# New places in a hand-written schedule: 72 of 564 side jobs of a fused attention and feed-forward kernel move by a fraction of a step to six steps

## The chip, the cores and the metric

The kernel runs on one core of one Trainium2 chip. The metric is the device time in microseconds of one execution, as the median of the runs. The engines are named as in the profile: PE is TensorE's matmul side and PEld its weight loads, DVE is VectorE, ACT is ScalarE, POOL is GpSimd, and SP (or SPq) is SyncE, which issues every DMA of this kernel.

## The reference

Four batches of 1024 tokens of 256 channels, each with a context of 77 tokens, go through one cross-attention layer and one feed-forward layer:

```python
# x: (4, 1024, 256), ctx: (4, 77, 256), 16 heads of 16
h   = layernorm(x)
q   = h @ Wq
kv  = concat(ctx, h) @ Wkv                 # 1101 keys
dots = einsum(q, k) * 16 ** -0.5           # key j is hidden where j > i + 77
x   = x + (softmax(dots) @ v) @ Wout + bout
h   = layernorm(x)
h   = block_quant(h) @ block_quant(w_fc).T + b_fc      # 1024 hidden units, blocks of 32, 3 mantissa bits
h   = gelu(h)
out = x + block_quant(h) @ block_quant(w_proj).T + b_proj
```

`block_quant` rounds each block of 32 values to three mantissa bits under the exponent of the block's largest value.

## The kernel before, in words

**Attention sets the beat.** The work is cut into 196 steps, 48 for each of the first three batches and 52 for the last. A batch has two parts of 512 queries (the last batch: 512, 256 and 256), a part has four groups `g` of four heads (a block), and a block has a step for every 512 columns of key tiles. In each step PE multiplies keys with queries into the four banks of `psS` in two pairs (L1239), ACT takes the exponential of each pair into `probs` (L722), POOL zeroes what the mask hides (L665), and PE multiplies `probs` with the values into `psO` (L1224), one step behind, and two steps behind for the first step of a block.

**psO is one bank.** All steps of a block add up in it. When the block is done DVE copies it out (L992, item `o`: transpose, reciprocal, product, and for odd groups a second transpose into `attT`). The first product of the next block waits for that copy (`pe.wait_ge(o_copied, st.block)`, L1220). It stands in PE's loop two iterations after the block's last step, and everything behind it on PE waits with it.

**Side jobs.** All else is an item of a plan: `ln1`, `ln1root`, `ln1end` (first layer norm), `xnT` and `ctxT` (transposes), `qk` (projections, rounded into three bf16 parts by ACT, by DVE and POOL in `mid`, and laid out by `stack`'s DMAs), `v`, `over` and `flag` (a guard against overflow), `wout` (output projection and residual), `ln2`, `ln2root`, `ln2end` (second layer norm), `q2` and `q2end` (quantization of its result into `hq`'s first half), `xqT` (its transpose), `fc` (eight half tiles in one go, GELU by ACT, L795), `hamax` and `hq` (quantization of a hidden tile by DVE, L861 to L873), `hT` (a DMA transpose by SP, L623), `proj` (second projection, L1168, added to the residual by DVE, L1054), `store`, and the preparation of the weights (`lateloads`, `wquant`, `wload`, `wT`).

**The order is written by hand.** `PLACES` (L189 to L229) has a table for each batch. A number is the step before or after the batch's first at which the item is put; a negative one lies in the batch ahead. `plan()` (L233) sorts all items by that number and puts each into the first half (`PLAN[k, 0]`) or the second half (`PLAN[k, 1]`) of iteration `k`. Every engine walks the same plan in program order and does its share of each item:

```python
# PE, iteration k (L1254 to L1280)
score_pair(k + 1, 0); handle PLAN[k, 0]; score_pair(k + 1, 1); pv of PV_AT[k]; handle PLAN[k, 1]
# DVE, POOL and SP, iteration k
handle PLAN[k, 0] + PLAN[k, 1]
# ACT, iteration k (act_plan, L295): ctxT, xnT, v and qk stand one half later
exp(k + 1, 0); first half; exp(k + 1, 1); second half
```

So a number in `PLACES` sets two things: where in PE's stream of score and value products an item stands, and the order of items on each of the other engines. No engine passes an item that waits. Items that need PSUM take turns in three banks `psD` (`places()`, L310): `qk` has the third for itself after the start, `fc` goes round all three, the others alternate between two. PE waits until the one who read a bank last has freed it.

Two waits of SP matter below. `hT` of tile n waits until DVE has written `hq` of that tile and until PE has finished the `proj` that read the buffer before (`bank_full`, L622). `store` waits until DVE has added the result of its `proj` (`bank_free`, L626). SP runs its items in order as well.

Of the kernel before, what the change touches and what calls it, by code (L numbers as in the profile page):

```python
# [174 lines left out]
def diagonal(seg):  # L175
# [11 lines left out]
DONE_BEFORE = {"over": 1, "flag": 1, "xnT": 2, "ln1": 1, "ln1root": 1, "ln1end": 1, "v": 2}  # L187

PLACES = (  # L189
    {"lateloads": (6,), "ln1": (0,), "ln1root": (.5,), "ln1end": (1,), "xnT": (4, 4.5), "qk": (5.5, 7, 9, 11),  # L190
     "mid": (6.5, 8.5, 10, 12.5), "over": (13.35,), "flag": (13.35,), "stack": (8.6, 13), "v": (13.5, 16.25, 17.25),
     "o": (5, 9, 13, 17, 25, 32.75, 41, 49), "wquant": (14.5, 19, 29.1, 30.4), "wload": (17.25,),
     "wT": (22.5, 22.75, 23.5, 24.5, 32.25, 32.75, 33, 35), "xres": (7, 27.9),
     "xresb": (14.5, 15.5, 16, 17, 36, 37, 38, 39), "wout": (17, 20.75, 50.5, 51.25), "ln2": (22.75, 52),
# [14 lines left out]
     "proj": (40, 44, 69, 73.85), "store": (41, 44.1, 74, 74.75)},  # L209
    {"xin": (-67.5, -67.5), "cin": (-42,), "ctxT": (-31.85,), "ln1": (-63,), "ln1root": (-59,), "ln1end": (-57.25,),  # L210
     "xnT": (-44, -39.75, -36, -31), "qk": (-24, -20.95, -18, -14.5, -10, -4.5, -1.95, 5, 9.5),
     "mid": (-22.5, -19, -17, -11, -8, -2.25, 0, 7, 11), "over": (-7, 13.5), "flag": (-5.5, 13.75),
     "stack": (-15.5, -1, 2, 13), "v": (-15, -6.5, .5, 6, 0), "o": (5, 9, 13, 17, 25, 33, 41, 49), "xres": (7, 28),
     "xresb": (14.5, 15.5, 16.5, 17.5, 35.75, 37, 38, 39), "wout": (17.5, 20.25, 49.5, 52), "ln2": (23.75, 52),
# [4 lines left out]
     "store": (41, 44.1, 71.5, 74.75)},  # L219
    {"xin": (-67.5, -67.5), "cin": (-42,), "ctxT": (-31.85,), "ln1": (-59,), "ln1root": (-59,), "ln1end": (-53.25,),  # L220
     "xnT": (-44, -39.75, -36, -31), "qk": (-24, -20.95, -18, -14.5, -9.5, -4.6, -1.95, 5, 9.5),
     "mid": (-22.5, -19, -17, -11, -7.5, -2.25, 0, 7, 11), "over": (-7, 13.5), "flag": (-5.5, 13.75),
     "stack": (-15.5, -1, 2, 13), "v": (-15, -6.5, .5, 6, 0), "o": (5, 9, 13, 17, 21, 25, 29, 33, 38, 43, 48, 53),
     "xres": (7, 27.5), "xresb": (14.5, 15.5, 16.5, 17.5, 30, 31, 32, 33), "wout": (17.5, 21.25, 33, 54),
# [1084 lines left out]
```

How the kernel before makes its waits and increments, by code:

```python
        def flag_of(eng, b, c):  # L491
            eng.wait_ge(flag_ready, CHUNKS * b + c + 1)
            n = CHUNKS * b + c
            return eng.value_load(flag_i[0:1, n:n + 1], min_val=0, max_val=1) > 0
# [38 lines left out]
            def stack(b, c, hf):  # L534
                before = [((b - 1) * CHUNKS + 1) * GROUPS + 2 * hf + 1, 2 * (2 * (CHUNKS * b + c) + hf - QB) + 1]
                if max(before) > 0:
                    sp.wait_ge(pair_scored, 2 * (BLOCK_END[max(before)] + 1))
                lo, hi = (0, FIRST_KEYS) if c == 0 else (CTX, FIRST_KEYS)
                sp.wait_ge(parts_ready, NUMBER["qk", b, c, "q", hf] + 1)
                for s in range(SLOTS):
                    sp.dma_start(q_stack[DH * s:DH * (s + 1), q_place(b, c, hf), :, :],
                                 q_parts[:, hf, Q_PART[s], :]).then_inc(stacked[hf], 16)
                sp.wait_ge(parts_ready, NUMBER["qk", b, c, "k", hf] + 1)
                for s in range(SLOTS):
                    sp.dma_start(k_stack[DH * s:DH * (s + 1), HH * hf:HH * (hf + 1), CHUNK * c + lo:CHUNK * c + hi],
                                 k_parts[:, hf, K_PART[s], lo:hi]).then_inc(stacked[hf], 16)
# [1 line left out]
            def place_guard(k, guarded):  # L549
                st = STEPS[k]
                with sp.If(guarded):
                    sp.wait_ge(guard_split, (st.block + 1) * 4)
                    for s in range(3):
                        sp.dma_start(q_heads(GUARD + s, GUARD + s + 1, st)[:, :, st.at:st.at + st.nq],
```

## Time and profile before

| what | value |
|---|---|
| runs | 661.85, 661.31 and 658.93 us, median 661.31 us |
| profiled execution, own time | 661.85 us |
| its span in the profile | 660.1 us |
| mean granted clock of TensorE | 0.944 |
| busy: PE, DVE, ACT, POOL | 574.1, 430.6, 422.3, 219.9 us |

The span runs from the first to the last instruction of the profiled execution, and 1.75 us of that execution's time lie outside it. Busy shares are means over the whole span: the kernel begins with some 36 us ahead of the first exponential and ends with some 35 us of the last tiles' feed-forward after the last one, and in both PE is often idle. "Granted clock" is the share of full speed that TensorE was allowed; the page's row of clocks has it per slice.

### The profile page before, as it was taken

The page shows a single profiled execution, that of the slowest core. Times are in us where ns is not written, and L with a number is a line of the kernel's source. Part 1 is how long each engine was busy: PE and PEld are TensorE (multiplying, and loading weights), DVE is VectorE, ACT ScalarE, POOL GpSimd, SP SyncE. Part 2 cuts the span into 40 slices and gives each one's busy share as a digit, 9 for nine tenths or more (in the row PEclk, how much of TensorE's full clock was granted, in tenths as well). Part 3 has the DMA queues.
Part 4 walks back from the last instruction along what each step waited for, and adds up shares of the span by engine and source line. Part 5 has one row for each costly group of instructions (what it writes and reads, how often), then busy time and mean ns, then how long its engine had stood idle before and what let it go on. Part 6 is the DMA issues. An engine that isn't in the chain of part 4 may idle for free.

```text
span 660.1 us, 11818 instructions
## 1 busy us (share of the span) xinstructions
PE 574.1 (87%) x4147; PEld 268.0 (41%) x4147; DVE 430.6 (65%) x925; ACT 422.3 (64%) x555; POOL 219.9 (33%) x313
## 2 busy tenths in 40 slices
PE   8469789999998899998898799999999888898743
PEld 4213344333463335334354334444353355454321
DVE  4503877999848477679545677667239779584655
ACT  3156557678757686787456686887667845965800
POOL 3314511534325412524333611424336514212100
PEclk9969889999999899999899999999999989897976
DMA  5997902360099712347199612139199504111102
GB/s 143 122 132 180 142 8 97 87 83 17 17 136 116 147 28 55 112 72 82 49 110 143 81 18 65 49 55 113 47 121 145 68 17 98 18 34 49 33 16 49
DMA packets 77703, 52.04 MB, mean 79 GB/s; under 512 B 37771, under 2 KB 77319, under 8 KB 77626
## 3 DMA queue, kind: packets, MB, share of 16 engines
q1 hardware_dynamic: 77626, 51.02, 49.0%
q8 instruction: 47, 0.77, 0.6%
q14 instruction: 30, 0.25, 0.2%
HBM read 12.12 MB, written 4.19 MB: 25 GB/s over the span
## 4 chain that ended last, share of the span: by engine, by line
PE 49%; DVE 28%; issue 8%; ACT 5%; DMA 4%; SPq 3%; POOL 1%; DVEq 0%; ACTq 0%; POOLq 0%
PE psO L1224 14%; PE psS L1239 13%; PE psD L1139 4%; PE psD L1105 4%; DVE hid L872 4%; ACT probs L722 4%; PE psD L1159 3%; DMA k_stack<-k_parts 3%; DVE amax L861 3%; PE psD L1115 3%; PE psD L1168 3%; DVE hq L873 2%; DVE o_cols L992 2%; PE psD L1157 2%; DVE hid L853 2%
## 5 line engine op out<-in xcount | busy, mean ns | idle before, releaser
L722 ACT ACTIVATE probs<-psS 128x1024 f32<-128x1024 f32 (+4 forms) x392 | 329.4, 885 | 180.4 <-PE psS L1239 179.2
L1239 PE MATMUL psS<-q_stack,k_stack 99*128 99x512 bf16 (+5 forms) x1008 | 200.4, 315 | 21.9 <-ACT probs L722 8.4
L665 POOL TENSOR_SCALAR_AFFINE_SELECT probs<-probs 128x512 f32<-128x512 f32 (+2 forms) x164 | 106.2, 659 | 334.1 <-ACT probs L722 334.0
L1224 PE MATMUL psO<-probs,v_aug 128*17 128x512 f32 (+5 forms) x2016 | 177.5, 458 | 8.3 <-DVE o_cols L992 4.9
L1239 PEld LDWEIGHTS psS<-q_stack,k_stack 99*128 99x128 bf16 (+1 forms) x1008 | 80.9, 103 | 150.5 <-ACT probs L722 75.6
L1224 PEld LDWEIGHTS psO<-probs,v_aug 128*17 128x17 f32 (+1 forms) x2016 | 43.7, 97 | 93.3 <-issue 75.7
L861 DVE TENSOR_REDUCE amax<-hid 128x32 f32<-128x1024 f32 (+1 forms) x45 | 53.4, 1187 | 27.4 <-ACT hid L795 26.6
L872 DVE TENSOR_TENSOR hid<-hid,magic 128x1024 f32<-128x1024 f32 (+1 forms) x45 | 55.6, 1235 | 9.0 <-DMA hT<-hq 4.0
L873 DVE TENSOR_TENSOR hq<-hid,magic 128x1024 bf16<-128x1024 f32 (+1 forms) x41 | 53.8, 1312 | 1.4
L992 DVE STREAM_TRANSPOSE o_cols<-psO 128x512 f32<-128x512 f32 (+1 forms) x36 | 23.5, 654 | 47.7 <-PE psO L1224 47.1
L795 ACT ACTIVATE hid<-psD 128x512 f32<-128x512 f32 x64 | 36.8, 597 | 22.8 <-PE psD L1159 21.0
L1115 PE MATMUL psD<-wv,xcT 128*128 128x256 f32 (+1 forms) x160 | 40.4, 397 | 2.6 <-DVE k_most L946 2.1
L1139 PE MATMUL psD<-wo,attT 128*128 128x256 f32 x128 | 34.0, 412 | 9.1 <-DVE attT L1001 9.0
L1159 PE MATMUL psD<-wfc,xqT 128*128 128x512 bf16 x128 | 41.7, 410 | 0.0
L1168 PE MATMUL psD<-wproj,hT 128*128 128x256 bf16 x256 | 32.6, 281 | 8.3 <-DMA hT<-hq 8.3
L1105 PE MATMUL psD<-xcT,wk 128*128 128x512 f32 (+1 forms) x96 | 34.8, 492 | 0.0
L1115 PEld LDWEIGHTS psD<-wv,xcT 128*128 128x128 f32 (+1 forms) x160 | 29.7, 191 | 11.0 <-DVE k_most L946 2.9
L1006 DVE TENSOR_TENSOR x<-psD,x 128x512 f32<-128x512 f32 x16 | 11.1, 691 | 34.3 <-PE psD L1139 34.3
L1105 PE MATMUL psD<-xcT,wq 128*128 128x512 f32 x64 | 30.7, 601 | 1.2 <-ACT xcT L735 1.2
L1139 PEld LDWEIGHTS psD<-wo,attT 128*128 128x128 f32 x128 | 24.9, 202 | 16.6 <-issue 13.0
L1168 PEld LDWEIGHTS psD<-wproj,hT 128*128 128x128 bf16 x256 | 25.1, 100 | 14.7 <-issue 6.4
L945 DVE TENSOR_TENSOR rest<-psD,k_parts 128x512 f32<-128x512 f32 (+1 forms) x20 | 12.3, 614 | 28.2 <-ACT k_parts L775 27.5
(91 smaller groups left out, 546.7 us busy)
## 6 DMA issues: line engine op xcount, KB each, us to landing
q_stack<-q_parts SPq DMA_DIRECT2D x96, 128.0 KB, 4.8
k_stack<-k_parts SPq DMA_DIRECT2D x48, 147.2 KB, 7.8
k_stack<-k_parts SPq DMA_DIRECT2D x48, 128.0 KB, 5.5
x_in<-in_x_dram SPq DMA_DIRECT2D x8, 512.0 KB, 5.2
x<-in_x_dram SPq DMA_DIRECT2D x8, 512.0 KB, 5.3
out_dram<-x SPq DMA_DIRECT2D x16, 256.0 KB, 2.2
hid<-in_L_ffn_w_fc_dram SPq DMA_DIRECT2D x1, 1024.0 KB, 6.5
hid<-in_L_ffn_w_proj_dram SPq DMA_DIRECT2D x1, 1024.0 KB, 4.9
```

The source lines that it names most:

```text
L665: last = pool.affine_select(out=tile, in_=tile, compare_op=ALU.is_ge, fill=0.0, base=first - (P * t - CTX), pattern=[[0, GH], [1, m]], cha ...
L722: act.activation(probs[:, k % PB, 2 * pair:2 * pair + 2, 0:n], psS[:, 2 * pair:2 * pair + 2, 0:n], ACT.Exp, scale=DH ** -0.5).then_inc(pro ...
L861: chain(s, dve.tensor_reduce(size, v.rearrange("p (a k) -> p a k", k=BLK), AXX, ALU.max, apply_absolute_value=True), c0 + 1)
L872: chain(s, dve.tensor_tensor(vb, vb, const, ALU.add), c0 + 4)
L873: return dve.tensor_tensor(q.rearrange("p (a k) -> p a k", k=BLK), vb, const, ALU.subtract)
L1105: last = pe.matmul(dst, wt[:, kk, f * P:(f + 1) * P], xcT[:, kk, src:src + size], start=(kk == 0), stop=(kk == KD - 1))
L1115: last = pe.matmul(ps[0:rows, D * a:D * (a + 1)], xcT[:, kk, first:first + rows], wv[:, kk, :], start=(kk == 0), stop=(kk == KD - 1))
L1139: last = pe.matmul(ps[:, D * (t % 2):D * (t % 2 + 1)], attT[:, kk, P * (t % SUB):P * (t % SUB + 1)], wo[:, kk, :], start=(kk == 0), stop=( ...
L1159: last = pe.matmul(ps[:, :], xqT[:, t % SUB, kk, :], wfc[:, kk, cols], start=False, stop=(kk == KD - 1))
L1168: last = pe.matmul(ps[:, D * (t % 2):D * (t % 2 + 1)], hT[:, t % 2, kk, :], wproj[:, kk, :], start=(kk == 0), stop=(kk == KH - 1))
L1224: last = pe.matmul(psO[SQ * j:SQ * j + VW, first - st.q0:first - st.q0 + n], v_aug[0:rows, v_tile(st.b, st.c, t), GH * st.g + j, :], probs ...
L1239: last = pe.matmul(psS[0:rows, j, off:off + n], k_stack[0:ROWS, GH * st.g + j, P * t:P * t + rows], q_heads(0, ROWS, st)[:, j, first - CHU ...
```

## The change

Only numbers in `PLACES` change. No instruction is added or removed, no shape and no buffer changes; eight items swap the two shared PSUM banks. The diff, cut to the numbers that the prediction speaks of:

```diff
-    {"lateloads": (6,), "ln1": (0,), "ln1root": (.5,), "ln1end": (1,), "xnT": (4, 4.5), "qk": (5.5, 7, 9, 11),
+    {"lateloads": (2,), "ln1": (0,), "ln1root": (.5,), "ln1end": (1,), "xnT": (3, 4), "qk": (5, 7, 9, 11),
...
-     "o": (5, 9, 13, 17, 25, 32.75, 41, 49), "wquant": (14.5, 19, 29.1, 30.4), "wload": (17.25,),
+     "o": (5, 9, 13, 17, 28, 33, 41, 49), "wquant": (14.5, 19, 28.2, 29.5), "wload": (16.25,),
...
-     "x1b": (27, 28, 29, 30, 56, 57, 58, 59), "xqT": (30, 36.4, 58, 61), "fc": (37.5, 62),
+     "x1b": (27, 28, 29, 30, 56, 57, 58, 59), "xqT": (36, 36.5, 58, 61), "fc": (37.5, 62),
...
-     "store": (47.2, 50.5, 70, 75.5)},
+     "store": (47.1, 50.5, 70, 75.5)},
...
-     "qk": (-24, -20.95, -17.5, -14.5, -10, -6.75, .05, 5, 9), "mid": (-22.5, -20, -17, -12, -8, -2, 2, 6.9, 11),
+     "qk": (-24, -20.95, -17.5, -14.5, -10, -7, -1.45, 5, 9), "mid": (-22.5, -20, -17, -12, -8, -2, .5, 7, 11),
...
-     "o": (5, 9, 13, 17, 25, 33, 41, 49), "xres": (7, 28), "xresb": (14.5, 15.5, 16.5, 17.5, 36, 37, 38, 39),
+     "o": (5, 9, 13, 17, 28, 33, 41, 49), "xres": (7, 28), "xresb": (14.5, 15.5, 16.5, 17.5, 36, 37, 38, 39),
...
-    {"xin": (-67.5, -67.5), "cin": (-42,), "ctxT": (-31.85,), "ln1": (-63,), "ln1root": (-59,), "ln1end": (-57.25,),
+    {"xin": (-67.5, -67.5), "cin": (-42,), "ctxT": (-32,), "ln1": (-59,), "ln1root": (-59,), "ln1end": (-53.25,),
...
```

What that does to the order, by absolute step (`o(0,1,0)` is batch 0, second part, first group; "a" and "b" are the two halves of an iteration):

| items | before | after | passes on DVE or SP |
|---|---|---|---|
| `lateloads` | 6a | 2a | SP: ahead of both `xin` of batch 1 |
| `xnT(0,2)`, `xnT(0,3)`, `qk(0,1,q,0)` | 4a, 4b, 5b | 3a, 4a, 5a | nothing |
| `o(0,1,0)` | 25a | 28a | DVE: goes behind `mid`, `ln2end` and `q2` |
| `xqT(0,0)` | 30a | 36a | DVE: behind both `wquant` |
| `ln1(2)`, `ln1end(2)` | 33a, 38b | 37a, 42b | DVE: behind `xqT(0,1)`; behind `hamax(0,1)` |
| `qk`, `mid(1,1,k,0)` | 48a, 50a | 46b, 48b | PE: `qk` ahead of `proj(0,0)` |
| `store(0,0)` | 47a, after `hT(0,3)` | 47a, before it | SP: ahead of `hT(0,3)` |
| `mid(1,1,q,1)` | 54b | 55a | DVE: behind `ln2end(0,1)` and `q2(0,1)` |
| `o(1,1,0)` | 73a | 76a | DVE: behind `ln2root`, `proj(0,3)`, `mid`, `ln2end` and `q2` |
| `hq(1,5)` | 113b | 114a | DVE: behind `wout(2,0)` |
| `hq(2,5)` | 160a | 162a | DVE: behind `o(3,0,3)` and `wout(3,0)` |
| `wout(3,1)` | 165a | 164a | DVE: ahead of `hamax(2,7)` and `o(3,1,0)` |
| `hamax(3,1)`, `wout(3,2)` | 176b, 177a | 178a, 178b | DVE: `hamax` behind `o(3,1,3)` |
| `hq(3,3)`, `proj(3,0)` | 182b, 182b | 183a, 184a | DVE: `proj` behind `ln2end(3,1)` |
| `hamax(3,5)`, `hq(3,5)` | 191b, 192b | 192a, 193a | DVE: `hamax` behind `o(3,2,2)` |
| `proj(3,2)` | 196, after `wout(3,3)` | 195b | PE: ahead of the last value product and of `wout(3,3)` |

The remaining moved items shift by a half step or one step and keep their order on DVE, ACT, POOL and SP, apart from `wT`, `fc` and `xnT` items of the same kind as above and `store(1,2)`, which goes ahead of `hT(1,7)`.

## Rows read from the trace of the kernel before

**Rows 1.** The list of waits, whole span: who waited for whom, us, times, longest.
```profile
PE psD L1148 <- DVE hq L873: 20.0, 7, 7.6
...
PE psO L1224 <- DVE o_cols L992: 4.9, 2, 3.8
```
**Rows 2.** Timeline of DVE around step 27: start, us, what, [idle before].
```profile
117.30 0.72 DVE L992 STREAM_TRANSPOSE o_cols<-psO 128x512 f32<-128x512 f32 x1
...
119.25 1.58 DVE L853 TENSOR_SCALAR hid<-x,mean,rs 128x256 f32<-128x256 f32 x4
...
122.67 1.23 DVE L872 TENSOR_TENSOR hid<-hid,magic 128x1024 f32<-128x1024 f32 x1
```
**Rows 3.** Timeline of PE, same stretch and a little on.
```profile
118.16 1.91 PE L1224 MATMUL psO<-probs,v_aug 128*17 128x512 f32 x16 [1.01 <-DVE o_cols L992]
...
136.40 0.38 PE L1130 MATMUL psD<-ident_b,hid 128*128 128x128 bf16 x4 [1.03 <-DVE hid L873]
```
**Rows 4.** Timeline of DVE, steps 73 to 76.
```profile
260.00 0.72 DVE L992 STREAM_TRANSPOSE o_cols<-psO 128x512 f32<-128x512 f32 x1 [1.54 <-PE psO L1224]
...
264.73 1.59 DVE L853 TENSOR_SCALAR hid<-x,mean,rs 128x256 f32<-128x256 f32 x4
...
268.16 1.23 DVE L872 TENSOR_TENSOR hid<-hid,magic 128x1024 f32<-128x1024 f32 x1
```
**Rows 5.** Timeline of PE, steps 74 to 77.
```profile
263.64 1.91 PE L1224 MATMUL psO<-probs,v_aug 128*17 128x512 f32 x16
...
270.99 0.38 PE L1148 MATMUL psD<-ident_b,hq 128*128 128x128 bf16 x4 [1.26 <-DVE hq L873]
```
**Rows 6.** One window: length; busy (count) of PE, PEld, DVE, ACT, POOL; clock; DMA share; GB/s.
```profile
212.00:221.00 9.00, 5.64 (x26) 1.50 (x26) 5.43 (x8) 2.21 (x5) 6.70 (x7) 0.63 0.81 154
```
**Rows 7.** Timeline of SP and PE, steps 47 to 49.
```profile
180.92 2.62 SPq L623 DMA_TRANSPOSE hT<-hq  x2
...
187.64 1.91 PE L1168 MATMUL psD<-wproj,hT 128*128 128x256 bf16 x16
```
**Rows 8.** Instructions on tile hT: from issue to landing.
```profile
DMA to landing us min/median/max: 1.7/3.1/8.1
```
**Rows 9.** Timeline of DVE and PE, steps 55 to 59.
```profile
204.33 0.69 DVE L945 TENSOR_TENSOR rest<-psD,q_parts 128x512 f32<-128x512 f32 x1 [1.23 <-ACT q_parts L775]
...
215.36 0.59 PE L1148 MATMUL psD<-ident_b,hq 128*128 128x128 bf16 x4 [3.61 <-DVE hq L873]
```
**Rows 10.** Timeline of DVE and PE, steps 160 to 173.
```profile
529.04 0.70 DVE L992 STREAM_TRANSPOSE o_cols<-psO 128x512 f32<-128x512 f32 x1
...
531.38 3.44 PE L1139 MATMUL psD<-wo,attT 128*128 128x256 f32 x8 [2.42 <-DVE attT L1001]
...
560.38 0.61 PE L1148 MATMUL psD<-ident_b,hq 128*128 128x128 bf16 x8 [2.20 <-DVE hq L873]
```
**Rows 11.** Timeline of DVE and PE, steps 175 to 188.
```profile
571.25 1.21 DVE L861 TENSOR_REDUCE amax<-hid 128x32 f32<-128x1024 f32 x1
...
577.18 1.97 PE L1139 MATMUL psD<-wo,attT 128*128 128x256 f32 x8 [1.05 <-DVE attT L1001]
...
600.44 0.69 DVE L1054 TENSOR_TENSOR x<-psD,x 128x512 f32<-128x512 f32 x1 [1.62 <-PE psD L1168]
...
603.97 0.58 PE L1148 MATMUL psD<-ident_b,hq 128*128 128x128 bf16 x4 [2.70 <-DVE hq L873]
```
**Rows 12.** Timeline of DVE, SP and PE, step 191 to the tail.
```profile
616.28 7.09 SPq L623 DMA_TRANSPOSE hT<-hq  x2
...
618.58 0.45 DVE L992 STREAM_TRANSPOSE o_cols<-psO 128x256 f32<-128x256 f32 x1 [0.77 <-PE psO L1224]
...
627.60 1.97 PE L1139 MATMUL psD<-wo,attT 128*128 128x256 f32 x8 [1.71 <-DVE attT L1001]
...
631.98 0.69 DVE L1054 TENSOR_TENSOR x<-psD,x 128x512 f32<-128x512 f32 x1
```
**Rows 13.** Timeline of PE, step 4.
```profile
48.21 0.39 PE L1239 MATMUL psS<-q_stack,k_stack 99*128 99x512 bf16 x1 [2.67 <-issue]
```

More of the change, by code:

```diff
@@ L189 @@
 PLACES = (
-    {"lateloads": (6,), "ln1": (0,), "ln1root": (.5,), "ln1end": (1,), "xnT": (4, 4.5), "qk": (5.5, 7, 9, 11),
-     "mid": (6.5, 8.5, 10, 12.5), "over": (13.35,), "flag": (13.35,), "stack": (8.6, 13), "v": (13.5, 16.25, 17.25),
-     "o": (5, 9, 13, 17, 25, 32.75, 41, 49), "wquant": (14.5, 19, 29.1, 30.4), "wload": (17.25,),
-     "wT": (22.5, 22.75, 23.5, 24.5, 32.25, 32.75, 33, 35), "xres": (7, 27.9),
-     "xresb": (14.5, 15.5, 16, 17, 36, 37, 38, 39), "wout": (17, 20.75, 50.5, 51.25), "ln2": (22.75, 52),
+    {"lateloads": (2,), "ln1": (0,), "ln1root": (.5,), "ln1end": (1,), "xnT": (3, 4), "qk": (5, 7, 9, 11),
+     "mid": (6.5, 8.5, 10, 12.5), "over": (13.25,), "flag": (13.25,), "stack": (8.6, 13), "v": (13.5, 16.25, 17.75),
+     "o": (5, 9, 13, 17, 28, 33, 41, 49), "wquant": (14.5, 19, 28.2, 29.5), "wload": (16.25,),
+     "wT": (22.5, 22.75, 23.5, 24.5, 32.25, 32.75, 33, 35), "xres": (7, 28),
+     "xresb": (14.5, 15.5, 16, 17, 36, 37, 38, 39), "wout": (17, 21, 50.5, 51.25), "ln2": (23.75, 52),
@@ L195 @@
      "ln2root": (24.75, 54), "ln2end": (26, 55), "q2": (27, 55), "q2end": (28, 58),
[1 row of a table removed]
[1 row of a table added]
      "hamax": (39, 42, 44, 45.25, 62, 64, 67, 69), "hq": (40, 43, 45, 46.5, 63, 66, 68, 70),
[1 row of a table removed]
-     "store": (47.2, 50.5, 70, 75.5)},
-    {"xin": (-43.5, -43.5), "cin": (-41.5,), "ctxT": (-26.1,), "ln1": (-36, -28.25), "ln1root": (-36, -26),
-     "ln1end": (-30.25, -25.5), "xnT": (-29, -22.5, -22, -19.75),
-     "qk": (-24, -20.95, -17.5, -14.5, -10, -6.75, .05, 5, 9), "mid": (-22.5, -20, -17, -12, -8, -2, 2, 6.9, 11),
-     "over": (-7.75, 12.5), "flag": (-7.75, 13.75), "stack": (-15.5, 2, 2, 13), "v": (-16.75, -6, .5, 6, -5),
-     "o": (5, 9, 13, 17, 25, 33, 41, 49), "xres": (7, 28), "xresb": (14.5, 15.5, 16.5, 17.5, 36, 37, 38, 39),
[4 rows of a table removed]
-     "proj": (40, 44, 69, 73.85), "store": (41, 44.1, 74, 74.75)},
@@ L210 @@
-    {"xin": (-67.5, -67.5), "cin": (-42,), "ctxT": (-31.85,), "ln1": (-63,), "ln1root": (-59,), "ln1end": (-57.25,),
-     "xnT": (-44, -39.75, -36, -31), "qk": (-24, -20.95, -18, -14.5, -10, -4.5, -1.95, 5, 9.5),
[1 row of a table added]
+     "store": (47.1, 50.5, 70, 75.5)},
+    {"xin": (-43.5, -43.5), "cin": (-41.5,), "ctxT": (-26.25,), "ln1": (-36, -28.25), "ln1root": (-36, -26),
+     "ln1end": (-30.25, -25.5), "xnT": (-29, -23, -22, -21.25),
+     "qk": (-24, -20.95, -17.5, -14.5, -10, -7, -1.45, 5, 9), "mid": (-22.5, -20, -17, -12, -8, -2, .5, 7, 11),
+     "over": (-7.75, 12.5), "flag": (-7.75, 13.75), "stack": (-15.5, 2, 2, 13), "v": (-16.75, -6, .5, 6, -5),
+     "o": (5, 9, 13, 17, 28, 33, 41, 49), "xres": (7, 28), "xresb": (14.5, 15.5, 16.5, 17.5, 36, 37, 38, 39),
[4 rows of a table added]
+     "proj": (40, 44, 69, 73.75), "store": (41, 44.1, 70, 74.75)},
@@ L212 @@
+    {"xin": (-67.5, -67.5), "cin": (-42,), "ctxT": (-32,), "ln1": (-59,), "ln1root": (-59,), "ln1end": (-53.25,),
+     "xnT": (-44, -39.75, -36, -31), "qk": (-24, -20.95, -18.5, -14.5, -10, -4.75, -1.95, 5, 9.5),
      "mid": (-22.5, -19, -17, -11, -8, -2.25, 0, 7, 11), "over": (-7, 13.5), "flag": (-5.5, 13.75),
@@ L214 @@
      "xresb": (14.5, 15.5, 16.5, 17.5, 35.75, 37, 38, 39), "wout": (17.5, 20.25, 49.5, 52), "ln2": (23.75, 52),
[4 rows of a table removed]
[L219 to L222, printed above, removed]
-     "stack": (-15.5, -1, 2, 13), "v": (-15, -6.5, .5, 6, 0), "o": (5, 9, 13, 17, 21, 25, 29, 33, 38, 43, 48, 53),
-     "xres": (7, 27.5), "xresb": (14.5, 15.5, 16.5, 17.5, 30, 31, 32, 33), "wout": (17.5, 21.25, 33, 54),
[3 rows of a table removed]
-     "hT": (32.5, 35.5, 40.1, 40.15, 47.5, 49), "proj": (38.5, 42.75, 54), "store": (41, 44, 54.5)},
[4 rows of a table added]
+     "store": (41, 44.1, 70.5, 74.75)},
+    {"xin": (-67.5, -67.5), "cin": (-42,), "ctxT": (-32,), "ln1": (-59,), "ln1root": (-59,), "ln1end": (-53.25,),
+     "xnT": (-44, -39.75, -36, -31), "qk": (-24, -20.95, -18.5, -14.5, -10, -4.75, -1.95, 5, 9.5),
+     "mid": (-22.5, -19, -17, -11, -8, -2.25, 0, 7, 11), "over": (-7, 13.5), "flag": (-5.5, 13.75),
+     "stack": (-15.5, -1, 2, 13), "v": (-15, -6.5, .5, 6, 0), "o": (5, 9, 13, 17, 21, 25, 29, 33, 38, 43, 48, 53),
+     "xres": (7, 27.5), "xresb": (14.5, 15.5, 16.5, 17.5, 30, 31, 32, 33), "wout": (17.5, 20.25, 34.5, 54),
[3 rows of a table added]
+     "hT": (32.5, 35.5, 40.1, 40.15, 47.5, 49.5), "proj": (40, 42.75, 51.5), "store": (41, 44, 52)},
 )
```

24 rows, old and new, of the table PLACES are left out of this document.

## The prediction

> **What bounds the kernel now.** I read the list of waits first, then the timelines of PE and DVE side by side at each place where the plan changes. PE is the engine that seldom rests: it is busy for seven eighths of the span, and between the first exponential and the last nearly every idle microsecond of it has a name. The longest of those names in this case are two: PE waits for DVE to finish quantizing the second layer norm before it can transpose it (seven waits, 20.0 us together, the longest in the tail), and twice for DVE's copy of the attention accumulator, 4.9 us [rows 1]. So PE's stream of products sets the pace, and a place costs time where DVE or a DMA is late for it. A stall on PE is not made up later as long as PE's stream is dense, because the same products still follow.
>
> A stall also has a tail. After a wait of 2.42 us the eight output projections took 3.44 us; the same eight took 1.97 us elsewhere [rows 10, 12]. The granted clock says why: over 212 to 221 us, around a wait of 3.61 us, it averaged 0.63, so most of that stretch ran at 1.2 GHz instead of 2.4 [rows 6, 9]. After waits of 1.01 us sixteen products still took 1.91 us [rows 3, 5]. I take 1.5 us for such a tail, from 3.44 less 1.97, with 0 and 3.3 us as its ends (9.0 us at 0.63 loses 0.37 of 9.0).
>
> **The accumulator's copy, batch 0.** `o(0,1,0)` goes from 25 to 28, but the value product that waits for it stays in iteration 26. DVE now does `mid`, `ln2end` and `q2` first. In the trace DVE began this copy at 117.30, right after the work ahead of it, `ln2end` at 119.25 and the first pass of `q2end` at 122.67 [rows 2]. From 119.25 to 122.67 lie `ln2end` and `q2`, 3.42 us, and `mid` takes what lies between the copy's group (1.5 us) and 119.25, 0.45 us: the copy starts 3.9 us later. `wout(0,1)` goes behind one pair of scores, on which DVE waits, 0.5 us more. PE idled 1.01 us before; it will idle 5.4 us, 4.4 us more, and the tail adds 1.5. Behind the waiting product stand all scores, so ACT starves as well, and nothing covers it. Against it: PE is then late for DVE, so the wait of 1.03 us for `wquant` [rows 3] goes, but `ln1(2)` now stands at 37 and pushes `over` and `flag(1,0)` back by roughly 0.6 us. Sum +5.5 us, bounds +2.5 (only the copy's move less both short waits) and +8.
>
> **The same in batch 1.** Here DVE was not late: it stood idle for 1.54 us until the block was done, and began the copy at 260.00 [rows 4]. Now `ln2root`, `proj(0,3)`, `mid`, `ln2end` and `q2` come first. `ln2root` fits ahead of the block's end, but `proj(0,3)` binds: PE ends it after 262.8, then follow its addition and `mid` (1.05 us between 263.68 and 264.73), then 3.43 us of `ln2end` and `q2` [rows 4]. With `ln2root` out of the way the addition starts at 262.9, so the copy starts at 267.4 and ends at 268.2. PE wanted it at 263.64 [rows 5]: 4.6 us. The wait of 1.26 us at `xqT` a little later [rows 5] goes, since `q2end` then ends ahead of PE. With the tail, 4.6 - 1.3 + 1.5 = +4.8 us, bounds +2.3 and +6.5.
>
> The Trainium skill ("TensorE: Matmul & The Clock Gate", "HAM oscillation") puts the cost of a throttled stretch at its duration times one less 1.2/2.4, and says in "What's actually happening" that the affected matmuls vary from run to run with the phase of the monitor. By that rule the two tails together would lie anywhere between nothing and what two such stretches cost; the trace agrees with the size (clock 0.63) and shows no run-to-run variation, having one execution. My sum keeps the row's 1.5 us each.
>
> **SP around step 47.** `store(0,0)` goes ahead of `hT(0,3)`, so `hT(0,3)` waits for DVE's addition of `proj(0,0)` and one more issue; and `qk(1,1,k,0)`, four products and 1.9 us, goes ahead of `proj(0,0)` on PE, which delays all of SP against PE's stream. Both `hT` were issued from 180.92 to 183.54, one takes 3.1 us to land, and `proj(0,1)` wanted the second buffer in its second half, near 188.6 [rows 7, 8]. New: 183.5 + 1.9 + 1.7 + 3.1 = 190.2, up to 1.7 us late. DVE's later position can hide nothing here. Bounds 0 and +3; I take +1.0, between the two, as the landing may be as fast as the least in rows 8.
>
> **Waits that shrink.** `mid(1,1,q,1)` goes behind `ln2end` and `q2`. DVE stood 1.23 us for ACT at that point with the whole chain to `q2end` behind it, and PE waited 3.61 us for that chain [rows 9]. I take -1.2 us, bounds 0 and -3 (half of the slow stretch in rows 6 goes too). `hq(2,5)` goes behind `o(3,0,3)`: the block was done about 1.3 us before the copy began at 529.04, so the wait of 2.42 us shrinks to 1.1 and its slow stretch of 1.5 us goes [rows 10]. But the next wait, 2.20 us at 560.38, is for DVE's own chain [rows 10], which is ahead by only the 0.6 us that it idled less. So what PE gains in between it waits out there: -0.6 us, bounds 0 and -2.9.
>
> **Last batch, steps 176 to 188.** `wout(3,2)` goes half a step and more later and loses its wait of 1.05 us. `hamax(3,1)` (1.21 us and two small operations, 1.6 together, begun at 571.25) no longer fills the time in which DVE waited for the block; it is done before `wout`, but `hq(3,1)` stands behind the addition of `wout(3,2)`, which PE now reaches after two more pairs of scores and 32 value products, near 580.6 instead of 577.18: `hq(3,1)` ends about 3.5 us later. From there to 600.44 DVE had only 1.62 us to spare, and its chain ends in the wait of 2.70 us at 603.97 [rows 11]. 3.5 - 1.6 = 1.9, and `hT(3,3)` may bring 1 more: +2.0 us, bounds 0 and +3.5.
>
> **Tail.** `proj(3,2)` stood behind `wout(3,3)`, where PE had nothing else, and its addition (0.69 us at 631.98) stood in DVE's chain. Now it stands ahead of the last value product and waits for `hT(3,5)`. That was issued at the end of the SP row, 622.14 with 1.23 us; `hamax(3,5)` now starts behind `o(3,2,2)` (618.58 and 1 us) instead of ahead of it, which moves it by some 1.7 us [rows 12]. With 3.1 us to land [rows 8] that is 626.9; half of `proj`, 1 us, the last value product, 0.3, and the copy with two transposes, 1.65, put `wout(3,3)` at 629.9 instead of 627.60 [rows 12]. Less 0.7 for the addition: +1.6 us, bounds -0.7 and +3.
>
> **Steps 2 to 6.** A megabyte of `w_fc` is now moved while the key and query stacks of the second head half still land. PE's wait of 2.67 us in the middle of one pair of scores has no releaser in the program [rows 13]; it may be code loading, which more traffic would lengthen. Nearest row: that wait itself, so -2.7 to +2.7; I take 0. Everything else (`x1b`, `xresb`, `wT`, `fc` or `qk` by half a step, with equal order on the other engines) moves products within PE's dense stream: 0, bounds -2 and +2.
>
> **Sum.** 5.5 + 4.8 + 1.0 - 1.2 - 0.6 + 2.0 + 1.6 = 13.1 us on the profiled execution's own 661.85 us, 675.0 us. The median lies 0.5 us under it: 674.5 us.
>
> **The rivals.**
> - *The two copies alone* (chance 0.2). The waits are real, but the slow stretches, SP's delay and the last batch's shifts are hidden by waits that are there already: 4.4 - 1.0 + 0.6 + 4.6 - 1.3 = 7.3 us less the 1.8 of the shrinking waits, +5.5, 667 us. For it: DVE often has slack on the way to its next wait (1.62 and 1.54 us). Against it: rows 10 show a wait of half that length with its slow tail.
> - *All ends high* (0.15). The hT after `store` lands late, code loading is delayed, and the last batch pays both: the high bounds of these three, 3 + 2.7 + 3.5, instead of 3.0, make +19.3, 681 us.
> - *Not slower* (0.07). VectorE's chain from `ln2` to `xqT`, and not PE, is the bound between the blocks. Reordering a chain of fixed length costs nothing, PE just waits at `psO` instead of at `xqT`, and only the freed waits count: -1.2 - 2.9 - 1.05, about -5 us, 656 us. It decides where DVE's wait for PE after the copy would vanish by as much as PE's wait grows. For it: DVE had under 0.1 us idle around step 27. Against it: the waits that PE had at `xqT` and `wquant` are 1.26 and 1.03 us [rows 3, 5], a quarter of the new ones.
> - *The numbers do nothing* (0.03), because PE has slack that the modelled ends of its products conceal: 661 us.
>
> The likeliest, 674.5 us, has 0.55. Its own range is 669 to 680; with the neighbours the range is 664.5 to 681.5 us. About 0.5% is what a measurement of this kernel can tell from no change. Faster by over 0.5%: 0.06; within: 0.06; slower: 0.88.
>
> **What the new profile would show.** PE waiting for `o_cols` about 5 us near step 27 and 4 to 5 us near step 76, each with a stretch of clock below 0.7 behind it; the wait for `hq` at `xqT(1,0)` gone; the wait at `wout(3,0)` at about 1.1 us without a slow stretch; the last `wout` about 2 us later after the last exponential. The prediction is wrong if the list of waits has less than 7 us for `psO` on `o_cols`, or if that figure is there and the span has grown by less than 5 us.

## The result, and the profile after

The changed kernel takes 684.44 us (median of 4 runs, 680.23 to 686.13) where the kernel before takes 660.56 us (median of 4, 658.93 to 661.85). The ratio is 1.035, with an interval of 1.030 to 1.041, so it is slower by some 23 us. The forecast was 674.5 us with a range of 664.5 to 681.5: the sign was right, and the time lies above the range. The profiled execution took 684.1 us, its span is 682.3 us and TensorE's mean granted clock in it 0.931, against 660.1 us and 0.944 before.

To place the 22.15 us between the two spans I took the start of the first exponential of every step from both traces and subtracted. Where that lag jumps, the time was lost. It is a safer reading than a span alone, since two executions of one kernel differ by several us (more on that below). The tail counts from the end of the last exponential.

| place | lag it adds, us | predicted |
|---|---|---|
| steps 0 to 27 | +0.9 | 0 |
| steps 28 to 41, copy of batch 0 | +5.4 | +4.9 |
| steps 42 to 58, `flag` and SP | +2.9 | +1.6 |
| steps 59 to 60, `mid(1,1,q,1)` | -3.4 | -1.2 |
| steps 61 to 78, copy of batch 1 | +5.0 | +4.8 |
| steps 79 to 158 | +0.7 | 0 |
| steps 159 to 176, `hq(2,5)` and `xqT(3,0)` | +1.1 | -0.6 |
| steps 177 to 190 | +6.2 | +2.0 |
| tail | +3.4 | +1.6 |
| sum | 22.2 | 13.1 |

The prediction had its 0.6 us for `flag` inside the +5.5 of the first copy (4.4 + 1.5 - 1.0 + 0.6). Here it stands with `flag`, in the row of steps 42 to 58, where its cost falls.

The list of waits of the changed kernel answers [rows 1]; its columns are the same. PE's waits for the accumulator's copy have risen from 4.9 to 17.0 us. These are four waits: 4.73 and 4.58 us at the two moved copies, 3.95 us at step 184, and one of 3.74 us at step 91 that the kernel before had too (3.85 us).

```profile
PE psD L1148 <- DVE hq L873: 21.3, 6, 8.7
PE psO L1224 <- DVE o_cols L992: 17.0, 4, 4.7
```

The group of the value products on the page shows that they are also longer. They overlap, and keep PE busy for 184.3 us where it was 177.5. They are the same 2016 products, some of them at a lower clock.

```profile
L1224 PE MATMUL psO<-probs,v_aug 128*17 128x512 f32 (+5 forms) x2016 | 184.3, 473 | 20.3 <-DVE o_cols L992 17.0
```

**The two copies** stand in the timeline of PE (first fence) and of DVE (second), and answer [rows 2 to 5]. In both places DVE now does `ln2end` and the first half of `q2` (L853, L861) before it copies the accumulator (L992), and PE gets the bank some 0.9 us after the copy's start.

```profile
122.27 3.61 PE L1224 MATMUL psO<-probs,v_aug 128*17 128x512 f32 x16 [4.73 <-DVE o_cols L992]
...
273.98 3.53 PE L1224 MATMUL psO<-probs,v_aug 128*17 128x512 f32 x16 [4.58 <-DVE o_cols L992]
```

```profile
117.99 1.59 DVE L853 TENSOR_SCALAR hid<-x,mean,rs 128x256 f32<-128x256 f32 x4
119.72 1.22 DVE L861 TENSOR_REDUCE amax<-hid 128x32 f32<-128x1024 f32 x1
...
121.40 0.72 DVE L992 STREAM_TRANSPOSE o_cols<-psO 128x512 f32<-128x512 f32 x1
...
268.63 0.69 DVE L1054 TENSOR_TENSOR x<-psD,x 128x512 f32<-128x512 f32 x1 [2.31 <-PE psD L1168]
...
273.11 0.72 DVE L992 STREAM_TRANSPOSE o_cols<-psO 128x512 f32<-128x512 f32 x1
```

After each of the two waits the sixteen products take 3.6 and 3.5 us instead of 1.91. The windows over both places and over a third (columns as in [rows 6]) give the reason, a granted clock of 0.52, 0.62 and 0.57.

```profile
120.00:127.00 7.00, 4.73 (x21) 1.57 (x22) 5.14 (x8) 0.00 (x0) 0.43 (x1) 0.52 0.09 31
273.50:278.00 4.50, 4.03 (x19) 1.00 (x20) 3.46 (x5) 0.00 (x0) 0.00 (x0) 0.62 0.99 333
604.00:612.00 8.00, 3.79 (x36) 1.66 (x36) 7.45 (x18) 1.87 (x3) 2.84 (x2) 0.57 0.01 2
```

**Single waits of PE** that the prediction spoke of, in the order of its timeline: for `flag`'s scale ahead of step 42 (0.56 us before, second fence), at `xqT(0,2)` [rows 9], at `wout(3,0)` and at `xqT(3,0)` [rows 10].

```profile
168.90 0.24 PE L1122 MATMUL psD<-head_sum,qk_most 128*1 128x8 f32 x4 [2.01 <-DVE qk_most L954]
...
223.67 0.38 PE L1148 MATMUL psD<-ident_b,hq 128*128 128x128 bf16 x4 [2.74 <-DVE hq L873]
...
541.77 1.97 PE L1139 MATMUL psD<-wo,attT 128*128 128x256 f32 x8 [1.00 <-DVE attT L1001]
...
571.93 0.58 PE L1148 MATMUL psD<-ident_b,hq 128*128 128x128 bf16 x4 [4.50 <-DVE hq L873]
```

```profile
161.18 0.24 PE L1122 MATMUL psD<-head_sum,qk_most 128*1 128x8 f32 x4 [0.56 <-DVE qk_most L954]
```

**The last batch.** The timelines of PE and of DVE over steps 178 to 189 answer [rows 11]. The wait of 1.05 us at `wout(3,2)` (594.84) is gone. The wait of 2.70 us at `xqT(3,2)` (624.04) is the same to the hundredth. Between them stands a new wait of 3.95 us for the copy of block `o(3,2,0)`.

```profile
594.84 1.99 PE L1139 MATMUL psD<-wo,attT 128*128 128x256 f32 x8
...
608.78 3.38 PE L1224 MATMUL psO<-probs,v_aug 128*17 128x256 f32 x32 [3.95 <-DVE o_cols L992]
...
624.04 0.38 PE L1148 MATMUL psD<-ident_b,hq 128*128 128x128 bf16 x4 [2.70 <-DVE hq L873]
```

```profile
596.93 0.69 DVE L1006 TENSOR_TENSOR x<-psD,x 128x512 f32<-128x512 f32 x1 [5.83 <-PE psD L1139]
597.54 1.53 DVE L872 TENSOR_TENSOR hid<-hid,magic 128x1024 f32<-128x1024 f32 x1
599.10 1.23 DVE L873 TENSOR_TENSOR hq<-hid,magic 128x1024 bf16<-128x1024 f32 x1
600.24 0.74 DVE L824 BATCH_NORM_STATS2 stats<-x 128x6 f32<-128x256 f32 x2
...
605.74 1.23 DVE L872 TENSOR_TENSOR hid<-hid,magic 128x1024 f32<-128x1024 f32 x1
607.00 1.27 DVE L873 TENSOR_TENSOR hq<-hid,magic 128x1024 bf16<-128x1024 f32 x1
608.20 0.44 DVE L992 STREAM_TRANSPOSE o_cols<-psO 128x256 f32<-128x256 f32 x1
```

DVE is never idle for more than 0.1 us from the addition of `wout(3,2)` at 596.93 to the copy at 608.20 (the timeline has 28 instructions there, of which the fence shows the long ones), and the copy is last in the row.

**The tail** on ACT, PE and DVE answers [rows 12]. Each fence is one timeline.

```profile
642.72 0.49 ACT L722 ACTIVATE probs<-psS 128x154 f32<-128x154 f32 x2 [1.04 <-PE psS L1239]
```

```profile
644.46 2.21 PE L1168 MATMUL psD<-wproj,hT 128*128 128x256 bf16 x16
...
646.60 0.33 PE L1224 MATMUL psO<-probs,v_aug 77*17 77x77 f32 x8
...
648.94 3.38 PE L1139 MATMUL psD<-wo,attT 128*128 128x256 f32 x8 [2.02 <-DVE attT L1001]
```

```profile
646.70 0.69 DVE L1054 TENSOR_TENSOR x<-psD,x 128x512 f32<-128x512 f32 x1 [4.20 <-PE psD L1168]
647.31 0.44 DVE L992 STREAM_TRANSPOSE o_cols<-psO 128x256 f32<-128x256 f32 x1
```

### The profile page after: what moved, and what is told of

Same layout as the page of the kernel before. It is cut to its first block, busy times and chain, and to the rows that moved or that the text cites. A ratio compares the mean times of both kernels' runs of the same rounds, so it can differ in the third digit from the quotient of the medians.

```text
span 682.3 us, 11806 instructions
## 1 busy us (share of the span) xinstructions
PE 580.8 (85%) x4138; PEld 269.5 (40%) x4147; DVE 427.4 (63%) x925; ACT 422.0 (62%) x555; POOL 217.9 (32%) x313
## 4 chain that ended last, share of the span: by engine, by line
PE 50%; DVE 27%; issue 8%; DMA 5%; ACT 5%; SPq 3%; POOL 1%; DVEq 0%; ACTq 0%; POOLq 0%
PE psO L1224 15%; PE psS L1239 13%; PE psD L1105 5%; PE psD L1139 4%; DVE hid L872 4%; PE psD L1159 3%; ACT probs L722 3%; DMA k_stack<-k_parts 3%; PE psD L1168 3%; DVE amax L861 3%; PE psD L1115 3%; DVE o_cols L992 2%; DVE hq L873 2%; DVE stats L824 2%; PE psD L1157 2%
## 5 line engine op out<-in xcount | busy, mean ns | idle before, releaser
L1224 PE MATMUL psO<-probs,v_aug 128*17 128x512 f32 (+5 forms) x2016 | 184.3, 473 | 20.3 <-DVE o_cols L992 17.0
L861 DVE TENSOR_REDUCE amax<-hid 128x32 f32<-128x1024 f32 (+1 forms) x45 | 53.4, 1187 | 29.1 <-ACT hid L795 28.2
L992 DVE STREAM_TRANSPOSE o_cols<-psO 128x512 f32<-128x512 f32 (+1 forms) x36 | 23.5, 653 | 47.5 <-PE psO L1224 47.2
L697 POOL TENSOR_TENSOR x<-x,bproj_all 128x256 f32<-128x256 f32 x32 | 23.9, 754 | 24.0 <-DVEq L1023 24.0
```

Of the source, the lines that this page charges most:

```text
L861: chain(s, dve.tensor_reduce(size, v.rearrange("p (a k) -> p a k", k=BLK), AXX, ALU.max, apply_absolute_value=True), c0 + 1)
L1224: last = pe.matmul(psO[SQ * j:SQ * j + VW, first - st.q0:first - st.q0 + n], v_aug[0:rows, v_tile(st.b, st.c, t), GH * st.g + j, :], probs ...
```

## The experiments

Four kernels first, to split the loss by place; then four single edits of the last batch, where the prediction's sum had failed. The kernel before ran beside them, with a median of 661.82 us (7 runs) in the first set and 661.83 us (30 runs) in the second. The kernels of the first set ran four times each, those of the second nine to twelve times. A cost "by the ratio" is the measured ratio less one, times the kernel before.

**1. The changed kernel with both copies back.**

```diff
-     "o": (5, 9, 13, 17, 28, 33, 41, 49), ...      # batches 0 and 1
+     "o": (5, 9, 13, 17, 25, 33, 41, 49), ...
```

> The changed kernel with the two accumulator copies o(0,1,0) and o(1,1,0) put back to 25. Theory A (each copy's move costs its wait and the slow stretch behind it, and nothing recovers it): the profile of the changed kernel lags by 6.0 us at step 28 and 6.3 less 1.2 at steps 76 to 78, so 11 us less than the changed kernel's 684.4: about 673 us, with PE's wait for o_cols near steps 27 and 75 back under 1.1 us. Theory B (other moved items would have cost most of it anyway): 679 us or more.

Measured: 673.76 us, ratio to before 1.018 (1.010 to 1.027). Its span is 670.5 us, 11.8 less than the changed kernel's. Lags against that kernel: -6.2 us at step 28, -6.3 and +1.4 at steps 76 to 78. Its timeline of PE keeps the wait in the last batch:

```profile
530.91 2.99 PE L1139 MATMUL psD<-wo,attT 128*128 128x256 f32 x8 [1.00 <-DVE attT L1001]
...
596.99 3.36 PE L1224 MATMUL psO<-probs,v_aug 128*17 128x256 f32 x32 [3.96 <-DVE o_cols L992]
```

The two copies cost 10.7 us between the medians, as the sum had it, and about half of the loss lies elsewhere. With four runs of each kernel this cost is known to 6 or 7 us only; that it is the copies' rests on the lags, which fall at these two places.

**2. The kernel before with the two copies moved, and nothing else.**

```diff
-     "o": (5, 9, 13, 17, 25, ...                     # batches 0 and 1
+     "o": (5, 9, 13, 17, 28, ...
```

> The kernel before with only the two copies moved from 25 to 28. Theory A: +10 us, about 671 us, both waits between 4 and 5.5 us. Theory B: at most +5.5 us, 666 us.

Measured: 668.09 us, ratio 1.010 (1.005 to 1.016), between the two expectations. Its timeline of PE around step 27:

```profile
124.13 3.58 PE L1224 MATMUL psO<-probs,v_aug 128*17 128x512 f32 x16 [4.91 <-DVE o_cols L992]
```

The lags at the two places are what was predicted (+5.6 at step 28, and +6.8, +0.7 and -1.4 at steps 76 to 78), and the waits too (4.9 and 4.6 us). Yet its runs are only 6.9 us slower, by the ratio, with an interval of 3.2 to 10.6. In the profiled run 3.0 us came back at step 60: the wait at `xqT(0,2)` was 3.05 us instead of 3.61, and no low clock followed. Another 1.2 us came back over steps 159 to 163: `fc` took 1.7 us longer there, and then the wait at `wout(3,0)` was 1.10 us instead of 2.42, with no low clock behind it (more in the last section). The edit doesn't touch these places. The wait at `xqT(0,2)` is 3.05 us in experiments 5 and 8 too, and the one at `wout(3,0)` is 1.10 to 1.24 us in experiments 5 to 7, so I put this down to the execution and not to the edit. Whether the copies cost 7 or 10 us in the kernel before the runs can't tell.

**3. The changed kernel with the last batch's table back.**

```diff
-     "wout": (17.5, 20.25, 34.5, 54), "q2": (26.75, ...), "xqT": (28, 29.25, 43.5), "fc": (29.5, 44.5),
-     "hamax": (31, 34, 36, 38, 46, 48), "hq": (32, 35, 37, 39, 47, 49), "proj": (40, 42.75, 51.5), ...
+     "wout": (17.5, 21.25, 33, 54), "q2": (27.25, ...), "xqT": (28, 28.25, 43.5), "fc": (30, 44.75),
+     "hamax": (31, 32.5, 36, 38, 46, 47.5), "hq": (32, 35, 37, 38.5, 47, 48.5), "proj": (38.5, 42.75, 54), ...
```

> The changed kernel with the last batch's table of the kernel before. In the profiles the last batch accounts for about 10.7 us: 1.1 over steps 159 to 174, 6.2 over steps 178 to 190, 3.4 behind the last exponential. Theory A (the last table's own edits do it): 10 us less than 684.4, about 674 us. Theory B (DVE arrives late in the last batch because hq(2,5) of the third table moved, and the last table only passes it on): under 5 us less, 680 us or more.

Measured: 675.77 us, ratio 1.024 (1.018 to 1.031). The wait at step 184 is gone and the tail is 35.7 us again instead of 39.1. Its list of waits and its timeline of PE at `wout(3,0)` and `xqT(3,0)`:

```profile
PE psO L1224 <- DVE o_cols L992: 13.4, 4, 4.7
```

```profile
541.94 1.97 PE L1139 MATMUL psD<-wo,attT 128*128 128x256 f32 x8 [1.00 <-DVE attT L1001]
...
572.52 1.01 PE L1148 MATMUL psD<-ident_b,hq 128*128 128x128 bf16 x8 [4.50 <-DVE hq L873]
```

The table of the last batch costs 8.7 us in the changed kernel, between the medians. The second fence settles a smaller point: with `hq(2,5)` moved, the wait at `wout(3,0)` falls to 1.00 us and the one at `xqT(3,0)` rises from 2.20 to 4.50 us with the old table of the last batch too. By lag that rise is 4.3 us over steps 166 to 176, where the changed kernel has 3.8.

**4. The kernel before with the last batch's table of the changed one.**

```diff
-     "wout": (17.5, 21.25, 33, 54), "q2": (27.25, ...), "xqT": (28, 28.25, 43.5), "fc": (30, 44.75), ...
+     "wout": (17.5, 20.25, 34.5, 54), "q2": (26.75, ...), "xqT": (28, 29.25, 43.5), "fc": (29.5, 44.5), ...
```

> The kernel before with the last batch's table of the changed kernel. Theory A: +10 us, 671 us, with a wait of about 4 us for o_cols at step 184. Theory B: under +5 us and no such wait.

Measured: 675.96 us, ratio 1.022 (1.016 to 1.027): 14.3 us, more than the 10 expected. In its timeline of PE:

```profile
563.05 0.40 PE L1148 MATMUL psD<-ident_b,hq 128*128 128x128 bf16 x4 [3.62 <-DVE hq L873]
...
598.63 3.62 PE L1224 MATMUL psO<-probs,v_aug 128*17 128x256 f32 x32 [3.58 <-DVE o_cols L992]
```

By lags: +3.3 us over steps 166 to 176, nearly all of it around `xqT(3,0)`, +7.1 up to step 190, +3.4 in the tail. So this table alone does all that the last batch of the changed kernel shows from `xqT(3,0)` on. At `xqT(3,0)` itself it isn't the only cause: experiment 3 has the rise without this table, and with both edits it is no larger (3.8 us). That is one reason why the table costs 14.3 us here and 8.7 in experiment 3, where the rise stays.

**5. `hamax(3,1)` alone.** The kernel before with

```diff
-     "hamax": (31, 32.5, 36, 38, 46, 47.5),
+     "hamax": (31, 34, 36, 38, 46, 47.5),
```

> The kernel before with only hamax(3,1) moved from 32.5 to 34, behind the copy o(3,1,3). Steps 176 to 190 lost 6.2 to 7 us with the whole last table, most of it as a wait of 3.6 to 4.0 us for o_cols at step 184. Theory A (hq(3,1) behind the later wout(3,2) makes DVE late): hamax alone costs 0 to 1.7 us, its own length, and no wait over 1 us at step 184. Theory B (the filling of DVE's idle time by hamax was what kept it in time): +4 us or more, 665 us, with the wait at step 184.

Measured: 661.03 us, ratio 1.000 (0.998 to 1.002). There is no wait at step 184. Its `wout(3,2)` in the timeline of PE:

```profile
578.31 3.57 PE L1139 MATMUL psD<-wo,attT 128*128 128x256 f32 x8 [0.99 <-DVE attT L1001]
```

**6. `wout(3,2)` alone.**

```diff
-     "wout": (17.5, 21.25, 33, 54),
+     "wout": (17.5, 21.25, 34.5, 54),
```

> The kernel before with only wout(3,2) moved from 33 to 34.5. Theory A: hq(3,1) waits behind its addition, ends about 3.5 us later, and PE waits 3 us or more for o_cols at step 184 with a slow stretch behind: +5 us, 666 us. Theory B: PE loses its wait of 1.05 us at the old place and DVE catches up: 0 to -1 us.

Measured: 666.46 us, ratio 1.007 (1.005 to 1.009). Its profiled run is the fastest of its nine, 662.55 us, so the span is no measure of the cost here; the new wait is there. First the timeline of PE, then that of DVE:

```profile
578.92 1.99 PE L1139 MATMUL psD<-wo,attT 128*128 128x256 f32 x8
...
592.61 3.41 PE L1224 MATMUL psO<-probs,v_aug 128*17 128x256 f32 x32 [2.94 <-DVE o_cols L992]
...
606.14 0.58 PE L1148 MATMUL psD<-ident_b,hq 128*128 128x128 bf16 x4 [2.70 <-DVE hq L873]
```

```profile
580.95 0.69 DVE L1006 TENSOR_TENSOR x<-psD,x 128x512 f32<-128x512 f32 x1 [5.61 <-PE psD L1139]
...
592.02 0.44 DVE L992 STREAM_TRANSPOSE o_cols<-psO 128x256 f32<-128x256 f32 x1
```

In the kernel before, the copy and the product that waits for it stand like this, DVE first:

```profile
579.18 0.69 DVE L1006 TENSOR_TENSOR x<-psD,x 128x512 f32<-128x512 f32 x1 [2.15 <-PE psD L1139]
...
590.34 0.44 DVE L992 STREAM_TRANSPOSE o_cols<-psO 128x256 f32<-128x256 f32 x1
```

```profile
591.92 1.92 PE L1224 MATMUL psO<-probs,v_aug 128*17 128x256 f32 x32
```

From the addition to the copy it is 11.2 us before (590.34 - 579.18) and 11.1 us with the edit (592.02 - 580.95). That stretch of DVE is rigid, and how late `wout(3,2)` comes is passed on whole to the copy. PE gets the bank 0.6 us after the copy's start (592.61 - 592.02), so in the kernel before the spare time was 591.92 - 590.34 - 0.6 = 1.0 us.

**7. `proj(3,2)` alone.**

```diff
-     "proj": (38.5, 42.75, 54), "store": (41, 44, 54.5)},
+     "proj": (38.5, 42.75, 51.5), "store": (41, 44, 52)},
```

> The kernel before with only proj(3,2) and its store moved ahead of the last copy and wout(3,3). Theory A (the tail's loss of 3.4 us is proj standing ahead of the last value product): hT(3,5) lands earlier here than in the changed kernel, so the wait is short, and the tail loses proj's own 1.9 us and gives back 0.7 us of DVE: +1 to +2 us between the last exponential and the end. Theory B (what counts is that hT(3,5) is late, by hamax(3,5)'s move): 0.

Measured: 663.30 us, ratio 1.002 (1.000 to 1.004). In the profiled run, the fastest of its twelve at 655.86 us, the tail is 39.0 us where the kernel before has 35.7: 3.3 us more. Timelines of PE and of DVE:

```profile
616.33 1.92 PE L1168 MATMUL psD<-wproj,hT 128*128 128x256 bf16 x16
618.18 0.33 PE L1224 MATMUL psO<-probs,v_aug 77*17 77x77 f32 x8
620.52 3.58 PE L1139 MATMUL psD<-wo,attT 128*128 128x256 f32 x8 [2.01 <-DVE attT L1001]
```

```profile
618.28 0.69 DVE L1054 TENSOR_TENSOR x<-psD,x 128x512 f32<-128x512 f32 x1 [5.53 <-PE psD L1168]
618.89 0.44 DVE L992 STREAM_TRANSPOSE o_cols<-psO 128x256 f32<-128x256 f32 x1
```

`proj` doesn't wait for `hT` here. It costs its own 1.92 us ahead of the last value product, and its addition costs 0.6 us ahead of the copy. The eight output projections then run at the low clock, 3.58 us instead of 1.97. But the median is only 1.5 us above before, with an interval up to 2.8; the 3.3 us of the profile are not fully found in it, and that stays open.

**8. `hamax`, `hq` and `hT(3,5)` alone.**

```diff
-     "hamax": (..., 46, 47.5), "hq": (..., 47, 48.5), "hT": (..., 47.5, 49),
+     "hamax": (..., 46, 48),   "hq": (..., 47, 49),   "hT": (..., 47.5, 49.5),
```

> The kernel before with only hamax(3,5), hq(3,5) and hT(3,5) moved back by half a step. proj(3,2) stands behind wout(3,3), 4 us after the transpose lands. Theory A: 0. Theory B of e7: +1.5 us or more.

Measured: 661.28 us, ratio 1.001 (0.999 to 1.003), tail 35.7 us. No loss can be told from the noise. Its `wout(3,0)` in the timeline of PE, which the edit doesn't touch:

```profile
530.97 3.05 PE L1139 MATMUL psD<-wo,attT 128*128 128x256 f32 x8 [2.42 <-DVE attT L1001]
```

**What these leave open.** By their ratios the copies alone (6.9 us) and the last table alone (14.3 us) make 21.2 of the 23.3 us. The remaining 2 us would fit the new wait for `flag` and SP's steps 48 to 55, but each of these costs is uncertain by 3 to 4 us, and batches 0 to 2 without their copies were not run alone. The four single edits of the last batch add up to 6.4 us of the table's 14.3. The rise at `xqT(3,0)`, 3.3 us by lag, belongs to none of the four (the wait there is 2.20 to 2.22 us in experiments 5 to 8). By elimination it comes with the table's remaining numbers (`wout(3,1)`, `q2`, `xqT`, `fc` and others); no run shows which. For the other 5 us I have no run. `hq(2,5)` and `mid(1,1,q,1)` were not run alone in the kernel before. No version faster than the kernel before was found.

## Why the prediction was wrong

**The step that failed is the last batch, steps 176 to 188.** The prediction said that `hq(3,1)` would end 3.5 us later, that "from there to 600.44 DVE had only 1.62 us to spare, and its chain ends in the wait of 2.70 us at 603.97". The first half is right: the addition of `wout(3,2)` comes at 596.93 instead of 579.18, 17.75 us later where ACT's steps lag by 13.6, so 4.1 us late. The second half is wrong. The wait of 2.70 us is unchanged in the changed kernel and in experiment 6. The lateness never got there, because an earlier consumer caught it: the copy of `o(3,2,0)`, which stands in DVE's queue behind `hq(3,1)`, `ln2`, `hamax(3,2)`, `ln2root` and `hq(3,2)`. The copy starts 17.86 us later than before, while PE reached the product that needs it 12.91 us later (608.78 less the 3.95 of its wait, against 591.92). The difference of 4.95 less the spare 1.0 us is the wait of 3.95. Experiment 6 makes a wait at the same place, 2.94 us, with `wout(3,2)` alone, and the same sum gives it: the copy 1.68 us later, PE 2.25 us earlier, less the spare 1.0. Experiment 5 makes none with `hamax(3,1)`. By lag these steps cost +6.2 us for a term of +2.0, above its high bound of 3.5; what part of it is not this wait and the slow products behind it stays open. I had read DVE's slack from its idle time of 1.62 us at 600.44, which is behind the copy. What counts is the slack at the first item that PE takes from this stretch of DVE, and that was 1.0 us. The low clock behind the wait was not in the term either: 32 value products take 3.38 us instead of 1.92.

**The tail** had the right step and too small a size. The last `wout` starts 5.7 us after the last exponential's end (648.94 - 643.21) instead of 3.2, so 2.6 us later where 2.3 were predicted. Its 3.38 us instead of 1.97 add 1.4, and the addition that is no longer in DVE's chain gives 0.7 back: 3.3 us, of which the prediction had 1.6. The missing part is the low clock again, after a wait of 2.02 us. The reason given in the prediction, a late `hT`, doesn't matter: experiment 7 has the same tail with `proj` starting on time.

**The copies** were right, in mechanism and size: 5.4 and 5.0 us of lag for 4.9 (without the 0.6 for `flag`) and 4.8, with waits of 4.73 and 4.58 us where 5.4 and 4.6 were expected. The wait at `xqT(1,0)` is gone, as predicted. Experiments 1 and 2 tie both to the two numbers. By runs they cost 6.9 us in the kernel before and 10.7 in the changed one, two figures whose intervals overlap.

**`hq(2,5)`** went as described, with the size off. The wait at `wout(3,0)` is 1.00 us in all three kernels with this edit (the changed one, experiments 1 and 3). Less of that is gain than it seems, as without it the wait was 2.42 us in three profiles and 1.10 to 1.24 us in the four of experiments 2, 5, 6 and 7. The gain was more than waited out at `xqT(3,0)`, 4.50 us. The prediction left 0.6 us of gain over; with the rise around `xqT(3,0)` it was a loss of 1.1. The rise comes without the last table (experiment 3, where of the edits near it `hq(2,5)` is the likely cause, though it was not run alone) and without `hq(2,5)` (experiment 4), and the two don't add up.

**`mid(1,1,q,1)`**: the wait at `xqT(0,2)` is 2.74 or 2.75 us in the three kernels with this edit, and 3.05 to 3.62 us in the seven without it, a gain of 0.3 to 0.9 for the 1.2 predicted. The lag fell by 3.4 us there since the clock stayed high behind the wait: the sixteen value products took 1.83 us instead of 3.44. They took 1.83 us in experiments 2 and 7 too, without the edit, in experiment 7 behind a wait of 3.62 us. So no more than 0.9 us can be put down to the edit.

**SP and `flag`**: +2.9 us for +1.6. Of these 1.45 are the wait at `flag`, for which the prediction had 0.6 us in the term of the first copy. PE waited 0.69 us for the second `hT`, within the 0 to 1.7 us that the prediction worked out.

So the forecast of a loss stood on the right two waits. Of the 22.2 us between the profiles 13.1 were predicted; the miss of 9.1 us is the last batch (4.2), the tail (1.8), SP and `flag` (1.3), `hq(2,5)` (1.7), unassigned drift (1.6) and the copies (0.7), less 2.2 at `mid`. Those 2.2 us are luck, as they hang on the clock in two single executions.

## What to carry to other kernels

When an item comes later on an engine that works in order, walk down that engine's queue to the first thing that another engine takes from it, and compare slack there; idle time further on says nothing. An accumulator's copy with everything behind it on PE should stand ahead of quantization work that PE needs only later: here PE waited 4.6 and 4.7 us for the two moved copies, and the low clock came on top. Price each new wait of 2 us or more with that slower stretch, as an expected cost. All fourteen new waits of 2 to 5 us at steps 27, 76 and 184 and ahead of the last `wout`, over the profiles kept, had products behind them that took 3.3 to 3.6 us instead of 1.9 to 2.0; the waits of 2.7 to 3.6 us at `xqT(0,2)` had them in five profiles of ten.

## What the runs showed of the hardware

The low clock behind a wait is not a property of the wait. Eight output projections at `wout(3,2)` took 1.97 us behind a wait of 1.05 us in the kernel before [rows 11], and 3.57 us behind a wait of 0.99 us in experiment 5. At `wout(3,0)` they took 3.05 us in experiment 8 and 3.44 us before, both behind 2.42 us, and 1.97 and 2.99 us in the changed kernel and in experiment 1, both behind 1.00 us. The prediction's rule, that a wait of 1 us has no such tail and one of 2.4 us has one of 1.5, held only on average.

The wait itself moves too: 2.42 us in three profiles and 1.10 to 1.24 in four, at a place that none of these seven kernels changes. The low clock can come ahead of a wait and shorten it. In the three, `fc` just before it ran at full clock, and DVE began the copy for `wout(3,0)` without idling. In the four, the granted clock over `fc` was 0.76 or 0.77; PE came some 1.7 us later, DVE had caught up and stood idle for 0.6 to 1.5 us ahead of its copy. The same window in the kernel before and in experiment 5, columns as in [rows 6]:

```profile
516.00:523.40 7.40, 7.40 (x44) 2.79 (x42) 4.65 (x9) 6.40 (x11) 1.29 (x3) 1.00 0.82 83
```

```profile
518.80:526.00 7.20, 7.12 (x27) 2.88 (x26) 4.43 (x8) 4.54 (x9) 1.24 (x3) 0.76 0.83 84
```

The 30 runs of the kernel before lie between 655.92 and 665.56 us, and the time goes with the mean granted clock: 0.953 in the fastest, 0.941 in the slowest, and a correlation of -0.80 over the 30. "TensorE: Matmul & The Clock Gate" of the Trainium skill says in "What's actually happening" that the same kernel shows a different number of slow matmuls from run to run, depending on the phase of the monitor at its start; these rows show that the number differs in the middle of a kernel too. So an effect under 3 us can't be read from the spans of two profiles.
